# Layer 2 of a four-layer network as one block: norm, linear attention, projection and 4-bit feed-forward share one instruction stream

## The reference, cut to what matters

```
xn = layernorm(x)
q = elu(xn @ Wq.T + bq) + 1        # 16 heads of 8 channels
k = elu(xn @ Wk.T + bk) + 1
v = xn @ Wv.T + bv
kv = sum over tokens of k (x) v    # one 8x8 state per head and sequence
out = (q @ kv) / clip(q . sum(k), 1e-6)
attention = out @ Wo.T + bo
xq = fp4_quant_dequant(xn)         # blocks of 16, scale = max|.|/6, rounded to the 4-bit grid
h = silu(xq @ Wg.T) * (xq @ Wu.T)  # 352 wide, weights quantised too
feed_forward = fp4_quant_dequant(h) @ Wd.T
```

## Time and profile before

| | us |
|---|---|
| median of 3 runs | 1287.48 |
| lowest and highest | 1285.69, 1288.26 |
| the profiled execution, its own time | 1289.48 |
| its span | 1287.7 |

### The profile page before, as it was taken

The page is one execution under the profiler, slowest core; times in us unless marked ns, Lnnn a source line. Parts: engine busy times, 40 slices in busy tenths (PEclk is TensorE's granted clock), DMA queues, the critical chain, the costliest instruction groups (busy, mean ns, idle before and its releaser), DMA issues. The chain is left out here.

```text
span 1287.7 us, 20101 instructions
## 1 busy us (share of the span) xinstructions
PE 1068.0 (83%) x6743; PEld 544.1 (42%) x6743; DVE 847.6 (66%) x1584; ACT 636.3 (49%) x1311; POOL 131.8 (10%) x140
## 2 busy tenths in 40 slices
PE   4288999999999978955699999999988994647588
PEld 2211222222222214953145555555437773535458
DVE  7597878878878511555765656556434667779677
ACT  3303777777777766425045555555562333123352
POOL 4007000000000231730000000000000000002112
PEclk9656999999999989987789999999998998869699
DMA  3617222123123121735444314342100000000001
GB/s 98 194 32 171 74 54 72 44 54 74 42 54 72 32 74 30 244 122 196 121 93 99 69 49 94 88 92 55 37 1 1 5 1 1 1 1 1 2 1 34
DMA packets 64733, 82.98 MB, mean 64 GB/s; under 512 B 9868, under 2 KB 45349, under 8 KB 64614
## 3 DMA queue, kind: packets, MB, share of 16 engines
q1 hardware_dynamic: 56670, 57.93, 17.8%
q0 software_dynamic: 6864, 23.01, 6.0%
q10 hardware_dynamic: 1120, 0.95, 0.2%
HBM read 56.81 MB, written 17.90 MB: 58 GB/s over the span
## 5 line engine op out<-in xcount | busy, mean ns | idle before, releaser
L775 DVE TENSOR_REDUCE a_negmax<-a_mbank 128x1 f32<-128x1024 f32 (+7 forms) x512 | 488.8, 988 | 181.7 <-PE a_mbank L629 106.5
L741 ACT ACTIVATE a_probs<-a_ebank 128x512 f32<-128x512 f32 (+3 forms) x896 | 452.3, 554 | 310.9 <-PE a_ebank L647 153.7
L625 PE MATMUL a_mbank<-a_moving,a_still 128*128 128x512 bf16 (+3 forms) x896 | 280.3, 384 | 51.3 <-DVE a_negmax L775 19.7
L647 PE MATMUL a_ebank<-b_moving,b_still 128*128 128x512 bf16 (+3 forms) x896 | 282.8, 363 | 21.0 <-ACT a_probs L741 11.0
L666 PE MATMUL a_acc<-a_probs,a_slot_v 128*32 128x512 f32 (+3 forms) x1792 | 219.2, 561 | 3.9 <-ACT a_probs L741 3.6
L625 PEld LDWEIGHTS a_mbank<-a_moving,a_still 128*128 128x128 bf16 x896 | 73.0, 99 | 259.2 <-DVE a_negmax L775 130.2
L647 PEld LDWEIGHTS a_ebank<-b_moving,b_still 128*128 128x128 bf16 x896 | 85.5, 98 | 161.3 <-ACT a_probs L741 89.2
L654 PE MATMUL a_ebank<-a_bias_b,anti 128*128 128x240 bf16 (+2 forms) x864 | 118.0, 252 | 0.0
L654 PEld LDWEIGHTS a_ebank<-a_bias_b,anti 128*128 128x128 bf16 x864 | 78.5, 99 | 19.5 <-issue 1.7
L1503 POOL TENSOR_TENSOR f_hq<-f_u,f_big 128x704 f32<-128x704 f32 x8 | 11.1, 1384 | 618.0 <-DVE f_u L1382 618.0
L629 PE MATMUL a_mbank<-a_bias_a,anti 128*128 128x240 bf16 (+2 forms) x288 | 70.5, 257 | 0.0
(11 more groups left out here) (337 smaller groups left out, 1143.4 us busy)
## 6 DMA issues: line engine op xcount, KB each, us to landing
a_slot_v<-vo SPq DMA_DIRECT2D x16, 512.0 KB, 6.1
stack<-s_parts SPq DMA_DIRECT2D x16, 384.0 KB
b_moving<-stack SPq DMA_DIRECT2D x32, 192.0 KB, 4.5
b_still<-stack SPq DMA_DIRECT2D x32, 192.0 KB, 4.7
a_bias_b<-trow SPq DMA_DIRECT2D x32, 192.0 KB, 5.9
a_still<-stack SPq DMA_DIRECT2D x62, 96.0 KB, 2.4
a_moving<-stack SPq DMA_DIRECT2D x62, 96.0 KB, 2.5
stack<-s_parts SPq DMA_DIRECT2D x16, 256.0 KB
```

Of the source, the lines that this page charges most:

```text
L625: last = nc.tensor.matmul(mbank[:, bank, lo:hi], S.a_still[:, pr, jj, qt * P:(qt + 1) * P], S.a_moving[:, pr, lo:hi], start=True, stop=not ...
L647: last = nc.tensor.matmul(ebank[:, s % NE, lo:512], S.b_still[:, buf, pr, jj, kt * P:(kt + 1) * P], S.b_moving[:, buf, pr, 512 * h + lo:51 ...
L741: nc.scalar.activation(probs[:, g % 2, j, lows[g]:512], ebank[:, s % NE, lows[g]:512], ACT.Exp).then_inc(p_full, 1)
L775: nc.vector.tensor_reduce(negmax[:, pr, at:at + 1], mbank[:, use % 2, 0:(qt + 1) * P if causal else SEQ], AX.X, ALU.max, negate=True).then ...
```

## The change

The four phases become one block, `second_phase`. Within it:

- The norm goes by chunks of four tiles: four times four `bn_stats` and four `bn_aggr`, four square roots, and a reciprocal for each chunk.
- PE turns the feed-forward weights first, then for each chunk turns the tiles and makes the query, key and value products. The query product has one PSUM bank, so have the key product and the value product; the bank for values also takes the turned attention output.
- The map is now min(exp(z), 1) + relu(z). For queries ACT takes Exp and Relu with the bias straight from PSUM, and DVE joins them. For keys DVE adds the bias into `z`, ACT takes Exp and Relu of it, and DVE joins them. ACT copies the values out of PSUM without a bias; the value bias comes into the state afterwards, as the sum of the keys times the bias.
- The divisions, the turning and the output projection go by pairs of tiles instead of single tiles. POOL writes `xb` in four instructions.
- The quantisation of `S.xn` is cut into `scale`, `divide` and `quantise` for each half, laid between the maps and the divisions in DVE's queue; its last step, the product with the block scale, goes to POOL.
- The first gate/up product comes before the last attention outputs are projected; the rest of the feed-forward loop is the same, with its PSUM banks taken from the attention's.

```diff
@@ PE, second_phase
+            def project(c):
+                pe.wait_ge(tp_empty, place["x", c] + 1)
+                if c:
+                    pe.wait_ge(q_relu, c)
+                nc.tensor.matmul(lq[:, 0, :], S.wot[:, 1, :], S.xnT[:, chunk(c)], start=True, stop=True
+                                 ).then_inc(q_full, 1)
+                if c:
+                    pe.wait_ge(z_ready, c)
+                for i in range(CT):
+                    last = nc.tensor.matmul(lq[:, 1, tile(i)], S.xnT[:, tile(CT * c + i)], S.wot[:, 2, :],
+                                            start=True, stop=True)
+                last.then_inc(k_full, 1)
...
+            turn_gate(0)
+            turn_gate(1)
+            turn_down()
+            turn_x(0)
+            for c in range(CHUNKS):
+                if c + 1 < CHUNKS:
+                    turn_x(c + 1)
+                project(c)
+                if c == 2:
+                    keys(0)
...
+            for g in range(NG + 2):
+                if g == NG // 2 - 1:
+                    keys(1)
+                if g == NG // 2:
+                    turn_xq(2)
+                    turn_xq(3)
+                if g < NG:
+                    attend(g)
+                if 1 <= g <= NG:
+                    turn_y(g - 1)
+                if g == NG:
+                    pe.wait_ge(tp_empty, len(order))
+                    gate_up(0)
+                if g >= 2:
+                    project_y(g - 2)
@@ ACT, second_phase
+            def query(c):
+                act.wait_ge(q_full, c + 1)
+                if c >= 2:
+                    act.wait_ge(q_ready, c - 1)
+                nc.scalar.activation(expo[:, 0, c % 2, :], lq[:, 0, :], ACT.Exp, bias=S.b2col[:, 0:1]).then_inc(q_expo, 1)
+                nc.scalar.activation(relu[:, 0, c % 2, :], lq[:, 0, :], ACT.Relu, bias=S.b2col[:, 0:1]
+                                     ).then_inc(q_relu, 1)
+
+            def key(c):
+                act.wait_ge(z_ready, c + 1)
...
+                nc.scalar.activation(expo[:, 1, c % 2, :], z[:, c % 2, :], ACT.Exp).then_inc(k_expo, 1)
+                nc.scalar.activation(relu[:, 1, c % 2, :], z[:, c % 2, :], ACT.Relu).then_inc(k_relu, 1)
...
+            take_x(0)
+            for c in range(CHUNKS):
+                if c + 1 < CHUNKS:
+                    take_x(c + 1)
+                query(c)
+                value(c)
+                key(c)
@@ POOL, second_phase
+            for c in range(CHUNKS):
+                s = slice(CT * c, CT * (c + 1))
+                nc.gpsimd.tensor_tensor(xb[:, s], S.x[:, s], S.b_row[:, 5, :].unsqueeze(1).to_broadcast([P, CT, P]),
+                                        ALU.add).then_inc(biased, 1)
+            for i in range(2):
+                pool.wait_ge(xu_ready, i + 1)
+                nc.gpsimd.tensor_tensor(fp4_wide(xq[:, i * HALF:(i + 1) * HALF]), fp4_wide(tmp["u"][:]),
+                                        spread(tmp["big"][:]), ALU.mult).then_inc(xq_ready, 1)
@@ DVE, second_phase
+            def query(c):
+                dve.wait_ge(q_relu, c + 1)
+                V.scalar_tensor_tensor(qT[:, chunk(c)], expo[:, 0, c % 2, :], 1.0, relu[:, 0, c % 2, :], ALU.min,
+                                       ALU.add).then_inc(q_ready, 1)
...
+            def keys(b):
+                dve.wait_ge(kv_full, b + 1)
+                own.step(V.tensor_copy(total[:, b:b + 1], kp[:, 0, P:P + 1]))
+                own.done(V.tensor_tensor(state[:, b, P:P + HEADS], S.head_of[:],
+                                         total[:, b:b + 1].to_broadcast([P, HEADS]), ALU.mult))
+                V.scalar_tensor_tensor(raw[:], S.b_row[:, 4, :], total[:, b:b + 1], kp[:, 0, 0:P], ALU.mult,
+                                       ALU.add).then_inc(kv_taken, 1)
+                dve.wait_ge(kv_taken, b + 1)
+                own.settle()
+                V.tensor_tensor(state[:, b, 0:P], raw[:], S.same_head[:], ALU.mult).then_inc(state_ready, 1)
...
+            key_bias(0)
+            scale(0)
+            query(0)
+            key_bias(1)
+            key(0)
+            divide(0)
+            query(1)
+            key(1)
+            key_bias(2)
+            quantise(0)
+            query(2)
+            key(2)
+            key_bias(3)
+            keys(0)
+            scale(1)
+            query(3)
+            key(3)
+            divide(1)
+            for g in range(NG + 2):
+                if g < NG:
+                    if g == NG // 2 - 1:
+                        average(g)
+                        keys(1)
+                    else:
+                        average(g)
+                if g == 1:
+                    quantise(1)
+                if g >= 2:
+                    move(g - 2)
+            dve.wait_ge(moved, NG)
@@ network
-            norm_phase(nc, S, "n2")
-            with nc.sbuf_tensor("q2T", [P, TOK], F32) as qT, nc.sbuf_tensor("state", [P, BATCH, P + HEADS], F32) as st:
-                linear_phase(nc, S, "l2", qT, st)
-                project_phase(nc, S, "p2", S.wot[:, 4, :], S.b_row[:, 5, :], linear=(qT, st))
-            fp4_phase(nc, S, "f2")
+            second_phase(nc, S, "f2")
```

More of the change, by code:

```diff
@@ L1418, in fp4_phase @@
+        order = [("w", 0), ("w", 1), ("w", 2)] + [("x", c) for c in range(CHUNKS)] + [("xq", c) for c in range(CHUNKS)]
+        place = {what: i for i, what in enumerate(order)}
+        chunk = lambda c: slice(c * W, (c + 1) * W)
+        tile = lambda t: slice(t * P, (t + 1) * P)
         block = ctx.enter_context(nc.Block())
@@ L1473, in _, with take @@
[L1473 to L1479 removed]
+            def take(what, c):
+                act.wait_ge(tp_full, place[what, c] + 1)
+                return place[what, c] % 2
@@ new lines, in deviation, with take_x @@
+            def deviation(c):
+                act.wait_ge(var_ready, c + 1)
+                nc.scalar.activation(std[:, CT * c:CT * (c + 1)], mv[:, CT * c:CT * (c + 1), 1], ACT.Sqrt, bias=eps[:]
+                                     ).then_inc(std_ready, 1)
+            def take_x(c):
+                nc.scalar.copy(S.xnT[:, chunk(c)], tp[:, take("x", c), :]).then_inc(tp_empty, 1)
+            def query(c):
[5 more added lines that the diff above has]
+                                     ).then_inc(q_relu, 1)
@@ new lines, in take_xq, with take_y, silu @@
+            def take_xq(c):
+                nc.scalar.copy(xqT[:, chunk(c)], tp[:, take("xq", c), :]).then_inc(tp_empty, 1)
+            def take_y(g):
+                act.wait_ge(y_turned, g + 1)
+                if g >= 2:
+                    act.wait_ge(product, g - 1)
+                nc.scalar.copy(yT[:, g % 2].rearrange("p t c -> p (t c)"), yv[:, 0, 0:G * P]).then_inc(y_copied, 1)
+            def silu(t):
+                act.wait_ge(gu, t + 1)
+                if t >= 2:
+                    act.wait_ge(h_ready, t - 1)
+                nc.scalar.activation(sil[:, t % 2, :], gates[t % 2][:, 0, 0:F], ACT.Silu).then_inc(siluted, 1)
@@ new lines, in _ @@
+            for c in range(CHUNKS):
+                for t in range(CT * c, CT * (c + 1)):
+                    own.done(V.bn_stats(stats[:, t, :], S.x[:, t, :]))
+                own.settle()
+                for t in range(CT * c, CT * (c + 1)):
+                    last = V.bn_aggr(mv[:, t, :], stats[:, t, :])
+                last.then_inc(var_ready, 1)
+            for c in range(CHUNKS):
+                dve.wait_ge(std_ready, c + 1)
+                own.step(V.reciprocal(rstd[:, CT * c:CT * (c + 1)], std[:, CT * c:CT * (c + 1)]))
+                for t in range(CT * c, CT * (c + 1)):
+                    V.tensor_scalar(S.xn[:, t, :], S.x[:, t, :], mv[:, t, 0:1], rstd[:, t:t + 1],
+                                    ALU.subtract, ALU.mult).then_inc(xn_ready, 1)
```

459 lines of the change are left out of this document (233 added, 226 removed).

## The result

The changed kernel takes 1257.7 us in the median of 4 runs (1255.64 to 1259.71), the kernel before 1287.87 in 4 runs beside it: the ratio is 0.977, 95% interval 0.975 to 0.979. The profiled execution took 1255.64, its span is 1253.9 and its mean granted clock 0.922.

What follows compares the result with a forecast made beforehand. DVE was taken to set layer 2's pace up to the first quantising step of h: 46.9 us of work plus 8.6 of waits make 55.5 instead of 83.1. Saving 27.6 gives 1260 us, range 1256.5 to 1265.

Steps and rivals of the forecast that it cites:

- DVE's work: Layer 2 up to the first quantising step of h: DVE's steps sum to 46.9 us, against 60.3 before.
- Step 1, the first key product: At `key_bias(0)`: DVE waits 1.5 us for the first key product, with PE's clock low.
- Step 2, the chunk loop: In the chunk loop: DVE does not wait for ACT or PE, with 0.8 to 3.5 us to spare.
- Step 3, the lock: At `key(2)`: DVE is locked out by POOL's first 128x1024 product, 2.1 us; the second product costs nothing.
- Step 4, the pairs: At `average(3)` and `average(4)`: DVE waits 1.2 us at low clock, then 0.4 behind its own `keys(1)`, together 1.6.
- Step 5, the end: End of the pairs: `move(6)` waits 1.8 us, `move(7)` 0.1, then 1.5 for the second gate/up product and Silu; together 3.4.
- The loop behind: The feed-forward loop after the first quantising step of h: keeps its 61.2 us.
- The price of 27.6: Layer 2 up to the first quantising step of h: 55.5 us instead of 83.1, so 27.6 us saved.
- A (free run): Rival: no lock between DVE and POOL and the clock rises early; 32.1 us saved, 1255 us; chance 0.18.
- B: Rival: TensorE at 1.2 GHz until the feed-forward; 16.1 us saved, 1271 us; chance 0.22 with mixtures of late waits.
- C: Rival: Exp and Relu each need their own ACT table, 15 more loads; 8 to 12 us saved, 1278; chance 0.03.
- D: Rival: single PSUM banks lock PE, ACT and DVE into strict turns; 9 us slower, 1297 us; chance 0.03.

Runs made afterwards that it cites:

- warm: Changed kernel plus nine unread TensorE products, three before the first chunk is turned, six behind the second pair's attention product: 1255.07 us, ratio 0.972.
- quantise_last: Changed kernel with the quantisation of `S.xn` moved behind all maps and divisions in DVE's queue, same instructions: 1271.20 us, ratio 0.986.
- xq_by_dve: Changed kernel with the last quantising step of xn taken back from POOL to DVE for both halves: 1257.97 us, ratio 0.976.
- scale_beside_pool: Changed kernel with the second half's scale put straight behind `quantise(0)`, beside POOL's product, with its own buffer: 1256.74 us, ratio 0.973.
- gate_early: Changed kernel with the seventh pair's projection before the first gate/up product and the second gate/up product freed from waiting for the last additions: 1257.33 us, ratio 0.973.
- all_three: Changed kernel with the edits of scale_beside_pool, warm and gate_early at once: 1283.14 us, ratio 0.975 to the kernel before on the same chip.
- warm_v_by_dve: Changed kernel with the edits of warm and the value bias added by DVE again: 1286.18 us, ratio 0.977 to the kernel before on the same chip.
- all_three_b: The kernel of all_three with three more unread products behind the chunk loop and five instead of six later: 1280.79 us, ratio 0.974.

## Why the prediction was right

The forecast of 55.5 us for the front stage was 1.6 too long, and 1260 for the whole 2.3 too long, inside its range. The mechanism, DVE's work and five named waits, was right. That the waits sum to the 8.6 that was said is luck: the first was said 0.4 too small and the lock 0.4 too large, and two of them move with the clock. Its parts:

- **DVE's work.** 46.9 predicted, 45.3 measured (53.9 less the waits). Nearly all of it is the maps: I took 0.72 for each of twelve 128x512 instructions, busy time and a wait, but those that stand ready start 0.60 to 0.61 after one another although each is busy 0.69 (1075.39, 1076.00, 1076.60, 1077.20): 7.3 instead of 8.6. State 0.86 for one `keys` instead of 1.0, quantising 14.8 instead of 15.1; norm 9.7 where 9.9 was said, and pairs at 1.28 a step as said. The sixteen statistics ran beside POOL's four additions in 4.7, within the 4.8 that was said: POOL cost them nothing.
- **Step 1, the first key product.** Right in place and cause (1.5 said, 1.92 measured). The clock rose within the key product at about 1072, and warm shows it by removing it. The size is luck: the same products gave 1.40 to 2.14 in other runs.
- **Step 2, the chunk loop.** No wait over 0.1 in it, as said. quantise_last shows what holds this up: without the quantising steps between the joinings the same loop has seven waits instead of one.
- **Step 3, the lock.** One joining of 2.42, delaying DVE by 1.7 (2.1 said). xq_by_dve and scale_beside_pool show it. The second product, beside divisions and additions, cost nothing, as said.
- **Step 4, the pairs.** 1.06 and 0.52 against 1.2 and 0.4. warm removes the first (clock) and leaves the second: PE waits 0.45 at 1103.38 for the state from DVE's own `keys(1)`, and DVE then waits for PE's product. That is read from the releasers; no run moves it.
- **Step 5, the end.** 1.83 and 1.55 against 1.9 and 1.5; gate_early shortens this end by 0.86, with 0.9 expected.
- **The loop behind.** 61.9 before and after, from the first quantising step of h to the third layer's statistics.
- **The price of 27.6.** 29.2 in the profile; the medians of the runs shown differ by 30.2, with the spread of the layers before in it.

The rivals: A (free run) had both its conditions refuted by the lock and the two clock waits, which are there. B had the clock right and its consequence wrong: the clock fell twice, but was back within each phase (0.98 at 1072, 1.00 at 1100), and DVE met the last chunks without a wait. C is refuted: ACT runs eight Exp and eight Relu in turn with three table loads in all, none of them for Relu (L1470, L1478):

```profile
L1469 ACT ACTIVATE f_expo<-f_lq,b2col 128x512 f32<-128x512 f32 x4 | 2.8, 701 | 1.2 <-PE f_lq L1330 1.2
L1470 ACT ACTIVATE f_relu<-f_lq,b2col 128x512 f32<-128x512 f32 x4 | 2.8, 696 | 0.0
...
L1459 ACT ACT_TABLE_LOAD x1 | 1.3, 1283 | 0.0
L1469 ACT ACT_TABLE_LOAD x1 | 1.3, 1283 | 0.0
L1498 ACT ACT_TABLE_LOAD x1 | 1.3, 1283 | 0.0
```

That is the Trainium skill's rule (ScalarE: Activation LUTs, section "Table sets"), that relu stands in every set. D is refuted by a pair's step of 1.28 in the timeline (1105.46, 1106.73, 1108.01).

What the experiments add to the account: the cheaper map alone, with 6.4 us less work for DVE, shortened the stage by 2.0. It pays when other work on DVE stands between its steps, as in the one block. How the rest of the gain divides between the single block, the pairs and the work moved to POOL was not taken apart.

## What to carry to other kernels

Taking work off the engine that sets the pace pays in full only where it does not wait for another engine instead; price a fused stage as that engine's steps plus a short list of named waits, and use start-to-start times for instructions that stand ready. A phase of hand-overs between engines (maps, pairs) and a long chain of one engine (4-bit steps) belong interleaved: here that was worth 13.9 us against the same instructions one after the other. More waits in the maps are 5.3 of it and the bare hand-overs behind the chain 8.7; smaller terms cancel. Before handing DVE's step to POOL, look at what stands next in DVE's queue, and after a pause of TensorE look at the granted clock before blaming its work. Before adding up gains of single edits, see whether one of them lengthens a pause of TensorE that another relies on: 1.84 us became 3.1 by the moved scale and 5.5 by the value bias on DVE.

## What the runs showed of the hardware

- Beside a POOL product a DVE `tensor_scalar` of 128x64 took 0.90 us instead of 0.20 (scale_beside_pool); the reduction of 128x1024 took 1.21 with or without it.
- POOL pays for the lock too: its product took 2.31 or 2.32 us in each run in which it started inside a joining, 1.93 or 1.94 elsewhere.
- The same first products at the fallen clock made DVE wait 1.40, 1.41, 1.92, 1.93, 1.95 or 2.14 us in different runs: the moment at which the clock rises isn't fixed to the program.
- Unread products ran into a fallen clock and it rose while they ran: in warm from 0.50 (1062 to 1064) to 0.99, in all_three from 0.50 (1120 to 1122) to 0.81 and 1.00. What they cost depends on the time that PE has. Behind a pause of 1.84 us (warm) six of them left no wait; behind 3.11 and 5.45 us (all_three, warm_v_by_dve) they came late and at 0.50, with new waits of 2.5 and 5.1 us; in all_three_b three more filled the pause and the clock stayed at 1.00.
